# The first expert matrix as the stationary operand in the last 32 tiles of an attention and mixture-of-experts kernel

## What is computed

```python
hn2 = layernorm(x1, ln2_w, ln2_b).reshape(s * b, h)
rp = softmax(hn2 @ router_w.T)
topw, topi = top_k(rp, 2)
gates = sum(one_hot(topi, E) * topw[..., None], axis=1)
hmid = gelu(einsum('th,ehf->tef', hn2, w1))     # E, H, F = 8, 256, 512
y = einsum('tef,efh->th', hmid * gates[:, :, None], w2)
out = x + x1 + y
```

## Time and profile before

| what | us |
|---|---|
| median of three runs | 676.67 |
| the profiled execution | 678.21 |
| its span in the profile | 676.5 |
| PE busy | 587.2 (87%) |
| DVE busy | 442.1 (65%) |
| POOL busy | 431.6 (64%) |
| ACT busy | 359.9 (53%) |

### The profile page before, as it was taken

One profiled execution on the slowest core, in us unless ns is written; L12 is line 12 of the kernel. 1 busy time (PEld: TensorE's weight loads), 2 busy tenths in 40 slices (PEclk: granted clock), 3 DMA queues, 4 the chain that ended last, 5 costly groups with the idle time before them and its releaser, 6 DMA issues.

```text
span 676.5 us, 10759 instructions
## 1 busy us (share of the span) xinstructions
PE 587.2 (87%) x2808; PEld 415.2 (61%) x2808; DVE 442.1 (65%) x1031; ACT 359.9 (53%) x827; POOL 431.6 (64%) x502
## 2 busy tenths in 40 slices
PE   2679979788579998988998999899888999999992
PEld 2346656666356665766675676577566666766671
DVE  1266659788989999998968789899973500111110
ACT  4343552367346655654876777556444755444440
POOL 5886654873884588667589848862884584444442
PEclk9988997889889998998998999999889999999997
DMA  4466763430343134324135413342344445443421
GB/s 134 132 219 210 241 187 87 120 87 24 79 105 62 41 80 103 52 33 84 47 88 110 88 25 65 81 88 41 80 89 56 86 91 96 71 67 63 71 32 23
DMA packets 61773, 59.86 MB, mean 88 GB/s; under 512 B 17610, under 2 KB 57299, under 8 KB 61652
## 3 DMA queue, kind: packets, MB, share of 16 engines
q0 software_dynamic: 18288, 23.28, 20.7%
q1 hardware_dynamic: 43428, 35.91, 18.8%
HBM read 35.89 MB, written 27.46 MB: 94 GB/s over the span
## 4 chain that ended last, share of the span: by engine, by line
PE 40%; DVE 28%; POOL 15%; issue 7%; DMA 5%; ACT 3%; SPq 1%; POOLq 0%; DVEq 0%; ACTq 0%
PE b_y L1001 11%; PE b_h L986 11%; DVE qk_prod L864 7%; DVE sc L872 6%; POOL xs_d L440 6%; DVE pv_prod L932 6%; PE b_qk L1099 4%; PE b_at L1145 3%; PE b_t L993 3%; PE b_at L1092 2%; DMA out_dram<-y,tags 2%; POOL out_dram L475 2%; PE b_v L1099 2%; PE b_x L977 2%; DMA xs_d<-ring,slot_row 1%
## 5 line engine op out<-in xcount | busy, mean ns | idle before, releaser
L475 POOL DMA_INDIRECT out_dram<-y,tags x71 | 123.3, 1737 | 31.3 <-issue 21.3
L1001 PE MATMUL b_y<-w_s,hm_hmT 128*128 x568 | 136.3, 384 | 3.3 <-ACT y L574 1.9
L986 PE MATMUL b_h<-w_s,xT 128*128 x284 | 135.6, 601 | 0.6 <-ACT xT L535 0.3
L1001 PEld LDWEIGHTS b_y<-w_s,hm_hmT 128*128 128x128 f32 x568 | 103.6, 192 | 17.8 <-issue 6.6
L1145 PE MATMUL b_at<-ident,pv_prod 128*128 128x128 f32 x544 | 78.0, 297 | 32.7 <-DVE pv_prod L932 32.5
L1145 PEld LDWEIGHTS b_at<-ident,pv_prod 128*128 128x128 f32 x544 | 67.3, 153 | 41.8 <-issue 31.9
L864 DVE TENSOR_TENSOR qk_prod<-q,kv 128x1024 f32<-128x1024 f32 (+2 forms) x80 | 91.2, 1164 | 0.8
L932 DVE TENSOR_TENSOR pv_prod<-kv,pr 128x1024 f32<-128x1024 f32 (+2 forms) x80 | 86.9, 1133 | 1.4 <-PE b_at L1145 0.2
L699 DVE TENSOR_SCALAR y<-b_y,tags,live 128x256 f32<-128x256 f32 x24 | 13.1, 544 | 113.0 <-PE b_y L1001 113.0
L440 POOL DMA_INDIRECT xs_d<-ring,slot_row x64 | 71.7, 1121 | 18.9 <-issue 18.6
L872 DVE TENSOR_REDUCE sc<-qk_prod 128x64 f32<-128x1024 f32 (+2 forms) x80 | 82.1, 1051 | 0.3
(11 more groups left out here) (170 smaller groups left out, 1088.7 us busy)
## 6 DMA issues: line engine op xcount, KB each, us to landing
xin<-xs_d SPq DMA_DIRECT2D x71, 128.0 KB, 2.1
w_s<-in_L_ffn_w_dram SPq DMA_DIRECT2D x16, 512.0 KB, 4.3
xp<-in_x_dram SPq DMA_DIRECT2D x32, 128.0 KB
xud<-in_x_dram SPq DMA_DIRECT2D x32, 128.0 KB
out_dram<-x POOLq DMA_DIRECT2D x32, 128.0 KB, 3.2
xud<-in_x_dram SPq DMA_DIRECT2D x32, 126.0 KB
tags<-xs_d SPq DMA_DIRECT2D x71, 4.5 KB, 2.2
out_dram<-y,tags POOLq DMA_INDIRECT x71, 3.9
```

The lines of the kernel that those rows point to most:

```text
L475: pool.indirect_dma_start(out_rows, bass.IndirectOffsetOnAxis(ap=tags[:, j % NM, 0:1].bitcast(U32), axis=0), y[:, j % NY, :], None, comput ...
L986: mm = pe.matmul(b_h[:, :], xT[:, k * P:(k + 1) * P], w1_s[:, bass.ds(e * (HC * F) + k * F, F)], start=(k == 0), stop=(k == HC - 1))
L1001: mm = pe.matmul(b_y[:, 0:H], hmT[:, k * P:(k + 1) * P], w2_s[:, bass.ds(e * (FC * H) + k * H, H)], start=(k == 0), stop=(k == FC - 1))
```

## The change

From tile 39 (`TURNED`, the first that is turned behind the attention's loop) on, the first matmul has its operands exchanged: w1 is stationary in pieces of 128x128, `xT` moves in 128 columns, and the product comes out as hidden units by rows, which is how the second matmul wants it. The transposes of gelu's output, their eviction and `hmT`'s wait go for these tiles. `hm` and `hmT`, and the banks `b_h` and `b_t`, become two pairs that are used in turn. w1 is read from DRAM once per tile, 512 KB, into one of five buffers, the two of `qk_prod` and the three of `pv_prod`, which the attention no longer needs. SP issues these reads ahead of the tile's rows.

```diff
+        w1_part_in = [sem(f"w1_part_in{i}") for i in range(2 + NPV)]
...
+        TURNED = turned
...
+        w1_bufs = [qk_prod[:, 0, :], qk_prod[:, 1, :]] + [pv_prod[:, i, :] for i in range(NPV)]
+        NW = len(w1_bufs)
+
+        def w1_buf(j):
+
+            return w1_bufs[(j - TURNED) % NW]
+
+        def hidden(j):
+
+            return ((b_h, hm), (b_t, hmT))[(j - TURNED) % 2]
...
+            def w1_in(j):
+
+                if j == TURNED:
+                    sp.wait_ge(s["sc_ready"], G)
+                    sp.wait_ge(s["pv_used"], PIECES[G])
+                if j - TURNED >= NW:
+                    sp.wait_ge(s["h_ready"], j - NW + 1)
+                if j in FIRST:
+                    sp.wait_ge(s["tab_ready"], group_of(j) + 1)
+                e = sp.value_load(tab[0:1, j:j + 1], min_val=0, max_val=E - 1)
+                sp.dma_start(w1_buf(j).rearrange("p (o k f) -> p o k f", o=1, k=HC),
+                             w1[bass.ds(e, 1)].rearrange("o (k p) f -> p o k f", p=P)).then_inc(w1_part_in[(j - TURNED) % NW], 16)
...
                 while asked[0] < min(n, ALL) and rows_by(asked[0]) <= at:
+                    if asked[0] >= TURNED:
+                        w1_in(asked[0])
                     tile_in(asked[0])
...
             def gelu(j):
                 act.wait_ge(s["h_ready"], j + 1)
-                act.activation(hm[:, :], b_h[:, :], ACT.Gelu).then_inc(s["gelu_done"], 1)
+                if j < TURNED:
+                    act.activation(hm[:, :], b_h[:, :], ACT.Gelu).then_inc(s["gelu_done"], 1)
+                else:
+                    bank, dst = hidden(j)
+                    act.wait_ge(s["y_ready"], j - 1)
+                    act.activation(dst, bank[:, :], ACT.Gelu).then_inc(s["gelu_done"], 1)
...
-                if c is not None:
+                if c is not None and c < TURNED:
                     turned_h(c)
...
+            def up_turned(j):
+
+                bank, _ = hidden(j)
+                pe.wait_ge(w1_part_in[(j - TURNED) % NW], 16 * ((j - TURNED) // NW + 1))
+                pe.wait_ge(s["xT_sb"], j + 1)
+                pe.wait_ge(s["gelu_done"], j - 1)
+                if j == TURNED + 1:
+                    pe.wait_ge(s["hmT_sb"], TURNED)
+                w = w1_buf(j).rearrange("p (k f) -> p k f", k=HC)
+                for i in range(FC):
+                    for k in range(HC):
+                        mm = pe.matmul(bank[:, i * P:(i + 1) * P], w[:, k, i * P:(i + 1) * P], xT[:, k * P:(k + 1) * P],
+                                       start=(k == 0), stop=(k == HC - 1))
+                mm.then_inc(s["h_ready"], 1)
+
             def down(j, e):
-                pe.wait_ge(s["hmT_sb"], j + 1)
+                hmT = hidden(j)[1] if j >= TURNED else hm_hmT[:, F:2 * F]
+                if j < TURNED:
+                    pe.wait_ge(s["hmT_sb"], j + 1)
+                else:
+                    pe.wait_ge(s["gelu_done"], j + 1)
...
-                if c is not None:
+                if c is not None and c < TURNED:
                     turn_h(c)
-                if b is not None:
+                if b is not None and b < TURNED:
                     up(b, loaded[b])
+                if b is not None and b >= TURNED:
+                    up_turned(b)
```

## The result

The changed kernel takes 689.25 us (median of four, 684.16 to 689.71) against 676.11 us for the kernel before beside it: a ratio of 1.0156, interval 1.0115 to 1.0198. Ratios and their intervals are taken over fast runs alone and are not the quotient of the medians beside them, which is 1.0194 here. It is slower, by 13 us between the medians and by 10.5 by the ratio, and the time lies above the predicted range of 673 to 685. The profiled execution took 689.12 us with a span of 687.4.

The account below looks back on a forecast made before the run. The prediction took PE and the scatter-adds waiting for each other's landings as two nearly equal chains, the adds capping the gain. A 3.4 us gain and 5.2 us of later landings made +1.8 on 676.67: 678.5 us, range 673 to 685.

Parts of the forecast that it names:

- The sixteen pairs: Turned first matmul on PE: sixteen loads overlap sixteen matmuls at 0.11 us a pair, 1.76 us per tile.
- The third rival: On PE, the first matmul's loads don't hide: 3.1 us, a tile 5.0, about 704 us; chance 4%.
- the adds cap PE's gain: On POOL's chain of scatter-adds, only same-expert steps that waited for results shorten, so the gain is capped at 3.4 us.
- tile 47 takes back the early part: PE's gain on tiles 40 to 46, about 2.7 us, is spent waiting for tile 47's rows behind the scatters.
- PE's 12.5: Gain over 32 tiles, 0.39 us less each, if PE alone set the end: 12.5 us.
- The fourth rival: The adds are not the bound and PE's gain comes through: 664 us; chance 5%.
- a burst that begins during the add's 3.8 - 1.55 = 2.25 us costs some 0.2 us: On the DMA engines, a fetch starting during an add delays it some 0.2 us in 61% of cases, 0.12 us.
- 0.35 us per landing: Average delay fetches put on each add's landing; over 15 landing steps, 5.2 us.
- my upper bound of 0.9: Most a 512 KB fetch adds per landing, half the 1.8 us seen on x1's adds beside about 1 MB.
- The second rival: Fetches lock in step with the adds, each landing 0.6 us later or more: 686 us; chance 12%.
- the five result buffers are no bound: PE's lead over the adds grows by 9.4 us, while five steps of the adds are some 20.
- The first rival: Fetch and add share the DMA engines with little loss, under 0.2 us per landing: about 675.0 us; chance 30%.

Follow-up runs that it names:

- phase: The changed kernel with each fetch timed by a POOL mark just before an add, so issued 1.2 us behind the add's issue; 690.62 us, ratio 1.0183.
- early: The changed kernel with each fetch issued three tiles ahead of its rows in SP's order; 709.1 us, ratio 1.042.
- phase2: The changed kernel with each fetch timed by a POOL mark behind an add's issue, so issued 2.5 us behind that issue; 683.5 us, ratio 1.0076.
- the six kernels named above: The changed kernel, the kernel before with unread 512 KB fetches (684.68 us), and four variants of the changed kernel with SP's fetches reordered or retimed (683.5 to 690.62 us).

## Why the prediction was wrong

**Right: PE.** The sixteen pairs were forecast at 1.76 us and take 1.78; a tile was to take 3.71 us and takes 3.74. The loads of one first matmul in the changed kernel's timeline:

```profile
638.02 1.97 PEld L1040 LDWEIGHTS b_h<-xT,qk_prod 128*128 128x128 f32 x16
```

They run from 638.02 to 639.99 us, beside matmuls from 638.39 to 640.17, as the products' transposes did. The third rival (loads that don't hide, 704 us) falls. The Trainium skill, page "TensorE: Matmul & The Clock Gate", Part 3, lets a load overlap only where row groups differ; these loads are over all rows, and the trace does not agree. The same Part, under its mechanism, also lets a load into a background weight buffer go ahead of running matmuls, which would fit; no run here shows which buffer is used.

**Right: the adds cap PE's gain, and tile 47 takes back the early part.** Tile 47's rows were asked for at 557.79 us (557.62 before), PE waited 4.14 us for them, and add 42 left at 555.35 us instead of 555.91. Without the fetch's data the change gains 5.7 us of PE's 12.5. The fourth rival falls. The cap itself was put too low: I took six steps between tiles of one expert, 3.4 us, and there are seven. Add 66 is one as well; its step was 4.10 us before, because its result was late, which I read as the wait for a landing, and it is 2.14 us in the changed kernel. That makes some 5.4 us. The result of tile 66 in the timeline of the kernel before, ready only at 649.54 us, with add 66 issued at 650.85:

```profile
649.00 0.54 DVE L699 TENSOR_SCALAR y<-b_y,tags,live 128x256 f32<-128x256 f32 x1 [3.56 <-PE b_y L1001]
```

**Wrong: "a burst that begins during the add's 3.8 - 1.55 = 2.25 us costs some 0.2 us", and with it 0.35 us per landing, 5.2 us in all.** This is the step that failed. Without the data there are 15 landing steps from add 42 to 61 and they are shorter by (24.93 + 66.65) - (18.88 + 53.72) = 18.98 us: 1.27 us each, above my upper bound of 0.9. It was not that more adds met a fetch than I reckoned: I had 35 and 61 in a hundred, and from 560 us to the last fetch it was 9 of 14 steps (of 20 with the six behind it). It was what meeting costs: those nine steps took 6.24 us on average, the eleven others 4.40, and a landing step without fetches is 4.2. So a meeting cost 2.0 us, where I had priced it at half a burst of 1.29 us (0.65) if the add begins inside it, and at 0.2 if the burst begins during the add. Both halves of this are too small. By the packets a fetch of the changed kernel takes 2.0 to 4.5 us from its first to its last, 2.6 in the median, and not 1.29; and an add can wait out a whole fetch, as that of 600.78 us did. The bound from the adds of x1, halved with the bytes, was too low as well, 0.9 us against 1.27; whether the price is in proportion to the bytes, the runs with 32, 256 and 512 KB do not settle.

The sum by its bounds reached 690 us and so held the measured 689.25; the range that was stated left this end out. What I called no change, 1.35 us either way, rested on three runs of the kernel before, which in all its runs lay between 673.11 and 682.41 us.

Nine meetings at 2.0 us and eleven steps at 0.2 are 20.6 us. The same-expert steps give back 5.4, and the kernel before had four long steps of its own, of 4.7 to 5.9 us, together 4.1 us over 4.2, which must be taken off: 20.6 - 5.4 - 4.1 = 11.1, against 11.5 measured. For the fetches on the kernel before the same sum is 8 x 1.61 + 0.7 - 5.5 - 4.1 = 4.0, and its chain of adds is 4.0 us longer in the profiled execution (whose 681.1 us are 3.6 below that kernel's median). What makes those few long steps of the kernel before was not tried.

**The second rival had the time, and half the reason.** It gave 686 us at 12% for fetches that lock in step with the adds. An add that pays again and again is what the kernel "phase" shows, where 16 of 20 steps met a fetch. In the changed kernel the two do not lock; they drift through each other at 3.7 against 4.2 us, and right behind tile 47 the fetches come at SP's own pace. The timeline of SP there, tile 47's rows and three fetches:

```profile
557.79 0.34 SPq L345 DMA_DIRECT2D xin<-xs_d  x1
...
559.42 0.39 SPq L358 DMA_DIRECT2D pv_prod<-in_L_ffn_w_dram  x1
...
562.27 0.39 SPq L358 DMA_DIRECT2D qk_prod<-in_L_ffn_w_dram  x1
...
565.39 0.39 SPq L358 DMA_DIRECT2D qk_prod<-in_L_ffn_w_dram  x1
```

A fetch every 2.8 to 3.1 us, for a share of 0.93 of the engines from 560 to 580 us, is what no term of mine had: SP had been held at tile 47 and caught up. From add 42 to 47 the fetches' data cost 24.93 - 18.88 = 6.1 us; how much of that is the bunch was not shown, since early did not test it.

**Also wrong: "the five result buffers are no bound".** They were full nine times. It does not lengthen the chain of adds, for POOL never waited for a result there, but it takes PE's lead away and ties PE to the adds.

**The first rival** (little loss, 675 us) rested on engines that were busy 39% of the time. The Trainium skill, page "DMA: Bandwidth & Descriptors", section "Queues, rings and completion order", has an engine take turns between queues, a packet at a time. I took from it that an add would not wait out a burst. That does not follow: the same section puts a packet at some 9 to 17 descriptors, and by an estimate from that figure one turn can be a whole fetch, whose 256 packets by the profile's count are 16 to each of 16 engines. The trace has both cases, the add of 600.78 us that waited out its fetch and phase's add of 605.58 us whose packets alternate with the fetch's. With a fetch near its issue an add's step took at least 0.4 us and up to 3.6 us more than 4.2, and the mean DMA share was still below one.

## What to carry to other kernels

Where transfers that wait for each other set the end, look first at which transfers will be under way at the same moment, not at the mean share of the DMA engines: 0.82 was room enough for phase2's single adds at 4.2 us, and 0.83 not for the changed kernel's adds that a fetch met, at 6.2 us. Data that lay in SBUF already were better copied there by an engine with time to spare (671.0 us) than fetched again beside such a chain (689.3). And a step of a chain that waits for its input now and for a landing later must be told apart row by row before a gain is capped.

## What the runs showed of the hardware

- In the six kernels named above an accumulating indirect add of 128 KB lost 0.4 to 3.6 us against a step of 4.2 when a 512 KB read was issued between 1.2 us before and 1.4 us after it, and mostly nothing when it was issued 1.5 to 2.6 us after.
- Such an add's packets began 2.1 us after its issue where nothing was in the way, and 4.4 us after it behind a read's 256 packets (changed kernel, 600.78 us).
- In the changed kernel PE stood for 4.14 us ahead of tile 47, and then ran for a while at half its clock, 1.2 instead of 2.4 GHz. The stretch from 560 to 564 us (columns as above):

```profile
560.00:564.00 4.00, 3.51 (x10) 2.88 (x11) 0.00 (x0) 0.81 (x2) 3.34 (x3) 0.59 0.65 181
```

PE's timeline there, first of the changed kernel, then of the kernel before:

```profile
560.49 0.54 PE L1010 MATMUL b_x<-ident,xin 128*128 128x128 f32 x2 [4.14 <-DMA tags<-xs_d]
560.83 3.53 PE L1053 MATMUL b_y<-w_s,hm_hmT 128*128 x8
```

```profile
560.75 1.89 PE L1001 MATMUL b_y<-w_s,hm_hmT 128*128 x8
```

The mean granted clock is 0.59 from 560 to 564 us, and the eight second matmuls that began at 560.83 us took 3.53 us. In the kernel before, where only PE's loads waited, 0.80 us, they took 1.89 and the granted clock of these 4 us was 1.00. It cost the end nothing that a row shows, as POOL waited for landings and not for results.
